# Probabilities times V: eight matmuls of 256 columns per key tile in place of four of 512

## The reference

```
q, k: 2 x 8 columns per head     v: 16 columns per head
a1 = softmax(q1 k1^T / sqrt(8)) v        a2 = softmax(q2 k2^T / sqrt(8)) v
o  = rms_norm(a1 - lam * a2) * norm_w * (1 - 0.2),   then o @ w_proj^T + b_proj
```

## Time and profile before

| | |
|---|---|
| time, median of 3 runs | 1919.76 us (1917.24 to 1920.37) |
| profiled execution, its own time | 1921.88 us |
| its span, first to last instruction | 1920.0 us |
| mean granted TensorE clock | 0.979 |
| busy: PE, DVE, ACT, POOL | 1806.7, 1519.4, 1382.7, 482.4 us |
| attention stage | about 590 to 1870 us |

### The profile page before, as it was taken

How to read it: one execution, slowest core, us unless ns; L and a number is a source line. 1 busy time by engine, 2 the same in 40 slices (tenths; PEclk the granted TensorE clock), 3 DMA queues, 4 the chain that set the end, 5 groups by cost and what they waited for, 6 DMA issues and landing times.

```text
span 1920.0 us, 39207 instructions
## 1 busy us (share of the span) xinstructions
PE 1806.7 (94%) x11714; PEld 767.9 (40%) x11714; DVE 1519.4 (79%) x1768; ACT 1382.7 (72%) x2688; POOL 482.4 (25%) x884
## 2 busy tenths in 40 slices
PE   6573999999999999999999999999999999999888
PEld 5222999998782222222222222222222222222226
DVE  5763444445649999999999999999999999999933
ACT  4122555554348888888888888888888888888783
POOL 0475000000001344354453444511111111111310
PEclk9796999999999999999999999999999999999899
DMA  8587332222103111111111111100101101001002
GB/s 296 179 252 220 109 96 92 88 87 88 34 17 113 38 32 44 34 38 39 31 42 35 35 42 31 41 24 21 28 20 25 24 20 29 20 24 25 11 1 88
DMA packets 98639, 120.54 MB, mean 63 GB/s; under 512 B 18820, under 2 KB 72708, under 8 KB 97556
## 3 DMA queue, kind: packets, MB, share of 16 engines
q1 hardware_dynamic: 92436, 103.01, 18.3%
q0 software_dynamic: 6144, 16.79, 2.8%
HBM read 72.77 MB, written 46.40 MB: 62 GB/s over the span
## 4 chain that ended last, share of the span: by engine, by line
PE 87%; DVE 4%; issue 3%; ACT 3%; DMA 2%; SPq 1%; POOL 0%; ACTq 0%; DVEq 0%
PE banks L1073 26%; PE banks L1064 22%; PE banks L1027 11%; PE banks L1152 10%; PE banks L1130 9%; PE banks L1174 3%; ACT o_raw L666 2%; PE banks L984 1%; PE banks L1238 1%; DVE row_half L842 1%; PE banks L1112 1%; ACT arena_t L689 1%; SPq L383 1%; DVE arena_q L784 1%; DVE arena_q L779 1%
## 5 line engine op out<-in xcount | busy, mean ns | idle before, releaser
L842 DVE TENSOR_REDUCE row_half<-banks 128x2 f32<-128x1024 f32 x1024 | 1210.6, 1219 | 66.1 <-PE banks L1027 60.7
L689 ACT ACTIVATE arena_t<-banks 128x512 f32<-128x512 f32 x2048 | 1070.0, 603 | 160.7 <-PE banks L1064 160.5
L1064 PE MATMUL banks<-qk_ring 50*128 50x512 bf16 x2048 | 584.1, 387 | 10.6 <-ACT arena_t L689 7.2
L1073 PE MATMUL banks<-arena_t,v_ring 128*17 128x512 f32 x4096 | 543.9, 603 | 5.6 <-ACT arena_t L689 0.2
L1027 PE MATMUL banks<-qk_ring 48*128 48x512 bf16 x2048 | 421.1, 384 | 4.0 <-DVE row_half L842 3.5
L1064 PEld LDWEIGHTS banks<-qk_ring 50*128 50x128 bf16 x2048 | 141.6, 93 | 672.9 <-ACT arena_t L689 555.3
L493 POOL TENSOR_TENSOR inv_sum<-inv_sum,half_factor 128x16 f32<-128x16 f32 x64 | 13.8, 215 | 1235.4 <-DVE inv_sum L922 1235.4
L645 ACT ACTIVATE arena_t<-banks 128x512 f32<-128x512 f32 x128 | 76.6, 598 | 165.9 <-PE banks L1130 156.1
L1130 PE MATMUL banks<-rows_parts,w_parts 128*128 128x512 f32 x768 | 186.2, 398 | 2.0 <-POOL w_parts L472 2.0
L1152 PE MATMUL banks<-w_parts,hidden_parts 128*128 128x256 f32 x1536 | 188.1, 284 | 0.0
L1152 PEld LDWEIGHTS banks<-w_parts,hidden_parts 128*128 128x128 f32 x1536 | 185.3, 192 | 0.1
(11 more groups left out here) (127 smaller groups left out, 1036.2 us busy)
## 6 DMA issues: line engine op xcount, KB each, us to landing
qk_ring<-q_stack SPq DMA_DIRECT2D x768, 16.0 KB
slot_rows<-arena_r SPq DMA_DIRECT2D x8, 1024.0 KB, 9.0
arena_r<-slot_rows SPq DMA_DIRECT2D x16, 512.0 KB, 4.7
expert_rows<-arena_r SPq DMA_DIRECT2D x16, 512.0 KB, 3.2
q_stack<-arena_q SPq DMA_DIRECT2D x24, 256.0 KB
k_stack<-arena_q SPq DMA_DIRECT2D x24, 256.0 KB
qk_ring<-k_stack SPq DMA_DIRECT2D x128, 48.0 KB
v_heads<-arena_v SPq DMA_DIRECT2D x4, 1088.0 KB, 7.0
```

Source lines behind the costliest of these rows:

```text
L689: nc.scalar.activation(probs[:, kt % PSLOTS, q, :], banks[:, ST_BANKS[ring_place(4 * kt + q) % 3], :], ACT.Exp).then_inc(exp_done, 1)
L842: nc.vector.tensor_reduce(halves[:, :, j // 2], banks[:, pair:pair + 2, :], AX.X, ALU.max, negate=True).then_inc(smax_done, 1)
L1064: pe.matmul(banks[:, ST_BANKS[place % 3], :], qk_ring[rows, k % SLOTS, 1, kt * P:(kt + 1) * P], qk_ring[rows, k % SLOTS, 0, qh * CH:(qh + ...
L1073: mm = pe.matmul(banks[QUAD * q:QUAD * q + VP, OT_BANK, :], v_ring[:, k % SLOTS, kt, :], probs[:, kt % PSLOTS, q, :], start=(kt == 0), sto ...
```

## The change

In `pv`, each of the four matmuls over 512 columns becomes two over 256. The first half of the columns is done for all four pieces, then the second half. Only the very first matmul of a head into a partition quarter carries the start flag; for the second half at key tile 0 it is off. Waits and the semaphore are where they were: the wait ahead of the first matmul, the increment on the last.

```
-                for q in range(4):
-                    mm = pe.matmul(banks[QUAD * q:QUAD * q + VP, OT_BANK, :], v_ring[:, k % SLOTS, kt, :],
-                                   probs[:, kt % PSLOTS, q, :], start=(kt == 0), stop=(kt == TB - 1))
+                for half in range(2):
+                    columns = slice(half * CH // 2, (half + 1) * CH // 2)
+                    for q in range(4):
+                        mm = pe.matmul(banks[QUAD * q:QUAD * q + VP, OT_BANK, columns], v_ring[:, k % SLOTS, kt, :],
+                                       probs[:, kt % PSLOTS, q, columns], start=(kt == 0 and half == 0), stop=(kt == TB - 1),
+                                       skip_group_check=True)
                 mm.then_inc(pv_done, 1)
```

## The result

The changed kernel takes 1996.51 us (median of 4 runs, 1990.82 to 1998.35), the kernel before 1919.15 us in the same comparison. The ratio is 1.0399, 95% interval 1.0376 to 1.0422: 77 us slower, where 64 us were forecast. The profiled execution took 1998.35 us, with a span of 1996.4.

A forecast was written before the change was run, and what follows sets the result against it. TensorE, busy 94% of the span, was taken to bound the kernel, with the product with V on the critical path. Thirteen branches at 4.7 us (2.7 + 1.0 + 1.0) make 61, plus 3 for boundaries: 1984 us, range 1923 to 2040.

The forecast's parts named there:

- The likeliest case: TensorE's attention loop no longer fits its instruction store and is refetched at each branch: 1984 us, chance 0.70.
- halves cost some 3 ns per boundary: Product with V: two new boundaries on each of 512 key tiles add 3 us, from 0 to 14.
- the 14 at the top of the range: Product with V: 14 ns at each new boundary, making 14 us in all.
- The longer loop no longer stays on the core: TensorE's attention loop grows from 1315 to 1827 instructions, too many to be held: 61 us over thirteen branches.
- the lower of the two counts: TensorE's loop of 1827 instructions touches eight or nine blocks; nine or ten must be held with the one ahead.
- a store has room for eight: TensorE's instruction store: eight 16 KB blocks taken as its room, the most the trace showed.
- Thirteen packets, or 26: Instruction queue between 736 us and the loop's end: 13 or 26 packets of 16 KB, 80 us apart.
- A gap of 2.7 us per branch: TensorE at each of thirteen taken branches: waits 2.7 us for a missing block, from 0.7 to 6.5.
- the 0.3 for queued work: TensorE at the branch: 0.3 us taken off the 3.0 us miss for old-turn work still queued.
- A second miss, 1.0 us: TensorE's loop, per branch: another missing block adds 1.0 us to the gap, at most 3.
- The clock, 1.0 us per turn: TensorE after a branch gap: a half-rate clock stretch costs 1.0 us per turn, from 0 to 2.4.

The follow-up runs named there:

- e5: Change in three of the loop's four heads, with 16 idle TensorE instructions run once ahead of the loop; ratio to before 1.0010, +2 us.
- e10: One loop head in four with matmuls cut into four pieces of 128 columns, loop head at a block's start; ratio to before 1.0054, +6 us.
- e1: Kernel before, matmuls untouched, with 16 idle instructions behind each product with V in the loop; ratio to before 1.0795, +152 us.
- e2: Kernel before, matmuls untouched, with 14 idle instructions behind each product with V in the loop; ratio to before 1.0576, +109 us.
- e7: Full change, with TensorE's loop opened with a hint of the branch back (`hint_back_edge=True`); ratio to before 1.0037, +7 us.
- e9: e2 with 16 idle TensorE instructions run once ahead of the loop; ratio to before 1.0049, +3 us in the medians.
- e3: The change inside the loop alone, the heads ahead of and behind it left as before; ratio to before 1.0536, +103 us.
- e8: e5 with the loops over `q` and `piece` exchanged, both halves of a piece in a row; ratio to before 1.0049, +10 us.
- e4: The change inside the loop for three of its four heads, the rest as before; ratio to before 1.0527, +100 us.
- e6: e3 with 16 idle TensorE instructions run once ahead of the loop; ratio to before 1.0321, +63 us.

## Why the prediction was right

The likeliest case was the one that came, on the side forecast; 64 us were forecast and 77 measured. By its steps:

- *The product with V is on the path that sets the end, and halves cost some 3 ns per boundary.* Right: 6 ns a tile for two boundaries in e5 (0.15 us per turn on 24 tiles), 0.99 us to the scores as before. 512 tiles make 3 us. Both the 3 ns and the 14 at the top of the range were my estimates, and no run shows the 14: e5 has 3 ns per boundary, and so has e10.
- *The longer loop no longer stays on the core.* Right, and by the lower of the two counts: no packet between 736 and 1780 us before, 111 in 732 to 1780 us after. e1 and e2 bring the cost without a changed matmul, e5 and e7 take it away with the changed matmuls in place, e9 takes it from e2. A store of eight blocks, the one ahead counted, fits which runs fetch and which don't: before touches seven (its head is the same nine instructions short of a block's end as e3's), which with the one ahead fill it; e5, e8, e9 and e10 touch seven; the changed kernel, e2, e4 and e6 eight, e1 and e3 nine. That a store has room for eight was my estimate, the most that the trace of before had shown; 151 packets with eight touched and one ahead, and 34 with seven, bear it out.
- *Thirteen packets, or 26.* Wrong, as was the estimate behind it of what is lost at a branch: about nine per turn (155 - 38 = 117 = 13 x 9, with 38 from e7, which fetches each block once). So a miss is not mended by one block: the loop touches eight, and with the one ahead all nine are fetched again in a turn (packets at 820.1, 823.0, 828.5, 838.0, 849.5, 861.0, 873.4, 883.5 and 894.8 us in the turn from 819.05). In which order the blocks in the store are replaced is not shown. The further packets cost little by themselves, since most of them come while TensorE is at work: at the branch shown the first starts at 1077.5, inside the gap, and the next at 1081.1, when TensorE has gone on. The count isn't settled to the last packet: e1 and e3 touch nine blocks each, and e1 fetches ten per turn on average (164 - 34 = 130), e3 nine.
- *A gap of 2.7 us per branch.* Measured 40.3/13 = 3.1, from 2.8 to 3.4 (3.38 in the branch shown): a little over the forecast, and near the 3.0 before the 0.3 for queued work is taken off.
- *A second miss, 1.0 us.* Right, and near in size: about 1.2. The 1.0 in the sum was my estimate, which no run shows as it stands; what they show is a second wait at each turn. In each of the thirteen turns the last two matmuls of the first product come late. The scores behind it start 2.61 to 3.59 us after its first matmul, where e6 has 1.84 at the same lower clock: 0.8 to 1.8 us. The matmuls' modelled lengths cover much of that, so that it shows as idle time only in part. Those two matmuls stand 41 instructions behind the head, where by the same count the second block begins (6062 ahead of the head there, and 6062 + 41 + 41 = 24 x 256); its packet starts at 1081.1 in the turn shown, 0.5 us after the first score. In e3, with nine instructions left, the stop is 1.8 to 2.5 us, and all of it is idle. e6, the same loop with its head near the start of a block, has none: its thirteen turns take 1107.1 us against 1124.7, or 1.4 per turn less. e3 against e6 prices the longer stop: (103 - 63)/13 = 3.1 us per turn, clock included.
- *The clock, 1.0 us per turn.* This was the term that was mis-sized most: about 1.5. e6 gives it without a second miss: in the thirteen turns TensorE is busy 1057.3 us, and 1037.7 in e7, which does the same work there without a gap. That is 19.5/13 = 1.5 us per turn. I had one half-rate stretch of 3.5 us to price (0.51 behind 2.54 us of idle time, and from one product to the next 3.60 us in place of 2.37, so 1.2 us lost) and took that as typical. In the changed kernel the one shown lasted 6.8 us (0.50 in 1079.3 to 1086.1), which is what a mean of 0.96 over a turn comes to (0.04 x 86.8 / 0.5 = 6.9), and such a turn is 1.5 us longer than one at 0.98.

Sum of what was measured in the thirteen turns, 81.9 us: 40.3 of gaps at the branches, some 16 of second misses (13 x 1.2), 2.6 by which e7's turns are longer too (the boundaries). That leaves 23, or 1.8 per turn, for the clock and for what a gap delays beyond its idle time (0.16 us at the branch shown). The 5.5 us by which the rest of the profiled execution was shorter bring the sum to the 76.4 of the span. So each step came, and each was a little too small: per turn the gap by 0.4 to 0.6 us, the second miss by 0.2, the clock by 0.5. That makes 18 us over the 64; the total missed by 13 only because the rest of the execution was shorter, which is luck.

## What to carry to other kernels

Count the instructions in a loop's body, passes and weight loads included, before cutting an operation in a written-out loop into smaller ones: one block more than fits cost 63 to 110 us here. If the page's instruction queue has packets in the loop's later turns, and the first instruction behind the branch sits idle on "issue", move the head to a block's start (+2 us in e5, +100 in e4), shorten the body (1315 instructions before, and no packet) or put the hint on the branch (+7 us in e7 in place of +77). Look at the distance of starts as well as at idle time: the second miss stood in no idle row of the branch shown, only in 2.61 us where 1.84 was due. And price a gap on TensorE with the slow clock that follows it; here the clock took some 20 us beside 40 us of gaps.

## What the runs showed that I had not expected

- Sixteen instructions that do nothing, ahead of a loop, were worth 98 us of 2019: e4 has 151 packets and turns of 87.0 and 88.4 us, e5 34 packets and turns of 80.37. By the count above the loop touches eight blocks in e4 and seven in e5.
- A hint on the branch did not only hide the fetch; it ended all fetching in the loop's later turns: no packet between 712 and 1778 us, and 38 in all against 155. By the same count eight blocks stayed there, where without the hint seven did (e5) and eight did not (e4, e6).
- Matmuls for different column quarters pass each other. Each fp32 matmul is two passes, and in the built program both passes of a piece stand ahead of the next piece's. In the product at 1218.05 us the first passes of the four pieces start within 0.02 us and the second ones 0.44 us later (1218.49 to 1218.51). In e8, with four passes in a row for each quarter, the first ones start within 0.04 us, and all sixteen stretch over no more than 1.08 us.
